# An attention and feed-forward stack on one core: the stages in another order on every engine

## What is computed

```
for i in range(DEPTH):                      # 6
    x = attn_layer(shift_tokens(x), Wqkv[i], q_scale[i], k_scale[i], Wo[i]) + x
    x = ffn_layer(shift_tokens(x), ln_g[i], ln_b[i], W1[i], b1[i], W2[i], b2[i]) + x

# attn_layer: 16 heads of 64; q, k are normed to length 1, scaled, rotated
sim = einsum('bhwie,bhwje->bhwij', bq, bk2) * 8        # 32 queries against 64 keys
attn = softmax(where(mask, -max, sim))
out = einsum('bhwij,bhwje->bhwie', attn, bv2)          # then out @ Wo
# ffn_layer: layer norm, hg = xn @ W1 + b1 (2 x 341 columns), a * gelu(gate) @ W2 + b2
```

## Time and profile before

| | |
|---|---|
| median of 3 runs | 3269.31 us (3269.1 to 3272.2) |
| the profiled execution, its own time | 3271.82 us |
| its span | 3270.0 us |
| PE busy | 3202.3 us, 98% |
| DVE busy | 2647.7 us, 81% |
| ACT busy | 2431.3 us, 74% |
| POOL busy | 2213.2 us, 68% |

### The profile page before, as it was taken

The page is one execution under the profiler, slowest core; times in us unless marked ns, Lnnn a source line. Parts: engine busy times, 40 slices in busy tenths (PEclk is TensorE's granted clock), DMA queues, the critical chain, the costliest instruction groups (busy, mean ns, idle before and its releaser), DMA issues. The chain is left out here.

```text
span 3270.0 us, 149708 instructions
## 1 busy us (share of the span) xinstructions
PE 3202.3 (98%) x62645; PEld 2538.3 (78%) x62645; DVE 2647.7 (81%) x6351; ACT 2431.3 (74%) x5028; POOL 2213.2 (68%) x1332
## 2 busy tenths in 40 slices
PE   7889999999999999999999999999999999999997
PEld 5668877877887887787787788778788778778875
DVE  5658888878888887888888888888888888888884
ACT  3347777777777777777777778778777777777774
POOL 5448767766776776676776677677677667767762
PEclk9989999999999999999999999999999999999999
DMA  4431111221211131111122111122111122112111
GB/s 160 161 128 51 45 43 43 55 88 48 56 46 42 47 98 48 53 45 43 46 87 63 48 50 46 38 82 71 49 44 48 43 62 87 53 45 53 50 45 37
DMA packets 110574, 200.00 MB, mean 61 GB/s; under 512 B 19280, under 2 KB 40784, under 8 KB 109136
## 3 DMA queue, kind: packets, MB, share of 16 engines
q1 hardware_dynamic: 107168, 185.17, 19.6%
q10 hardware_dynamic: 2736, 5.25, 0.5%
HBM read 41.45 MB, written 23.07 MB: 20 GB/s over the span
## 5 line engine op out<-in xcount | busy, mean ns | idle before, releaser
L438 POOL TENSOR_TENSOR qks<-work 128x1024 f32<-128x1024 f32 x384 | 909.9, 2370 | 134.9 <-issue 125.5
L446 POOL TENSOR_TENSOR qkr<-qks,rnorm 128x1024 f32<-128x1024 f32 x384 | 731.5, 1905 | 310.4 <-issue 223.0
L789 PE MATMUL psum<-wparts,xhi 128*128 128x512 f32 x2304 | 821.8, 438 | 11.9 <-POOL xlo L423 7.0
L573 ACT ACTIVATE sq<-psum 128x512 f32<-128x512 f32 x768 | 459.9, 599 | 301.4 <-PE psum L789 280.4
L454 POOL TENSOR_TENSOR probn<-prob,psumr 128x512 f32<-128x512 f32 x384 | 401.5, 1046 | 370.7 <-DVE psumr L1170 370.5
L1119 DVE TENSOR_REDUCE ssq<-sq 128x8 f32<-128x512 f32 x768 | 519.9, 677 | 4.3 <-ACT sq L573 4.2
L1146 DVE TENSOR_TENSOR work<-psum,rot 128x512 f32<-128x512 f32 x768 | 509.1, 663 | 1.8 <-POOL qks L438 1.8
L814 PEld LDWEIGHTS psum<-kT,qTs 64*32 64x32 f32 x24576 | 360.5, 107 | 145.2 <-issue 129.8
L789 PEld LDWEIGHTS psum<-wparts,xhi 128*128 128x128 f32 x2304 | 384.7, 191 | 101.2 <-issue 50.2
L789 PE MATMUL psum<-wparts,xlo 128*128 128x512 f32 x1152 | 459.7, 399 | 0.0
L1164 DVE TENSOR_REDUCE psumr<-prob 128x8 f32<-128x512 f32 x384 | 261.7, 682 | 243.4 <-ACT prob L625 240.8
(11 more groups left out here) (132 smaller groups left out, 5536.7 us busy)
## 6 DMA issues: line engine op xcount, KB each, us to landing
vsh<-vtok SPq DMA_DIRECT2D x384, 192.0 KB, 2.4
vsh<-vtok SPq DMA_DIRECT2D x384, 64.0 KB, 2.4
wsplit<-wstage SPq DMA_DIRECT2D x15, 1024.0 KB, 6.4
wparts<-wsplit SPq DMA_DIRECT2D x30, 512.0 KB, 3.9
xsh<-xs_in SPq DMA_DIRECT2D x192, 64.0 KB, 2.4
ff_x<-x_mid SPq DMA_DIRECT2D x96, 128.0 KB, 2.4
wraw<-Wqkv_dram SPq DMA_DIRECT2D x18, 512.0 KB, 4.3
rsplit<-rstage SPq DMA_DIRECT2D x5, 1024.0 KB, 3.8
```

The source lines that it names most:

```text
L438: pool.tensor_tensor(qks[:, :, :], rcos, rsin, ALU.add).then_inc(s["add_ready"], 1)
L446: pool.tensor_tensor(qkr[:, n % 2, :, :], qks[:, :, :], rnorm[:, :].unsqueeze(2).to_broadcast([P, 2 * OCT, DH]), ALU.mult).then_inc(s["qkr ...
L573: act.activation(sq[:, w * OCT:(w + 1) * OCT, :], bank[w].rearrange("p (h n) -> p h n", n=DH), ACT.Square).then_inc(s[("sqq_ready", "sqk_r ...
L789: mm = pe.matmul(out, xparts[xp][:, ti, :], wparts[:, SECTION_AT[w, oc], wp_, :], start=(k == 0), stop=(k == 2))
```

## The change

On all engines the loop calls its stages in another order, and some stages serve a unit one step later. On PE a step was: Q product, scores, turn Q, turn probabilities, K product, V product, turn K, attend, output. It becomes: turn Q, Q product, turn probabilities, K product, V product, turn K, scores, attend, output. `attend` and `output` are one step later. `ffn_tokens` moves from place 1 to place 2 and `ffn_features` stays at place 2 and so stands behind tokens, scores, attend and output of the same step; `ffn_up` stays at place 3 but moves from the step's end to behind the Q product; `ffn_down` moves from place 4 to place 7, between V product and turn K. `block_at` is rewritten so that a place may be 8 or more, and the loops run 8 steps longer. The waits' numbers follow the new distances; no wait is of a new kind. No instruction is added or dropped, but for a few rows that merge.

```diff
 def block_at(step, place):
-    b = step // UNROLL - 2
-    return b if step % UNROLL == place and 0 <= b < DEPTH * BLOCKS else None
+    b = (step - place) // UNROLL - 2
+    return b if (step - place) % UNROLL == 0 and 0 <= b < DEPTH * BLOCKS else None
...
-            x_low(0)
             global_inverse(2 * B - 1)
...
-            for step in range(STEPS + 2 * UNROLL):
-                if step:
-                    x_low(step)
-                probabilities(step - 5)
-                rotated(step - 1)
-                normed(step - 1)
+            for step in range(STEPS + 3 * UNROLL):
+                x_low(step - 2)
+                probabilities(step - 8)
+                rotated(step - 3)
+                normed(step - 3)
...
-            for step in range(STEPS + 2 * UNROLL):
-                ffn_renewed(renewed_at(step, 15))
-                mask_seeded(step - 3)
-                ffn_inverse(block_at(step, 2))
+            for step in range(STEPS + 3 * UNROLL):
+                ffn_renewed(renewed_at(step, 16))
+                mask_seeded(step - 4)
+                square(step - 1, 1)
+                values(step - 4)
+                ffn_inverse(block_at(step, 3))
                 x_high(step)
+                exponential(step - 5)
                 k_turned(step - 3)
-                attended(step - 6)
-                ffn_gates(block_at(step, 4))
                 ffn_affine(block_at(step, 3))
-                exponential(step - 4)
+                attended(step - 7)
+                q_turned(step - 2)
+                ffn_gates(block_at(step, 3))
+                inverse_norm(step - 1)
                 square(step, 0)
-                inverse_norm(step - 1)
-                q_turned(step - 2)
-                probabilities_turned(step - 5)
-                square(step, 1)
-                values(step - 3)
+                probabilities_turned(step - 6)
...
-            for step in range(STEPS + 2 * UNROLL):
+            for step in range(STEPS + 3 * UNROLL):
+                turn_q(step - 2)
                 projection(step, 0)
-                scores(step - 3)
-                turn_q(step - 2)
-                turn_probabilities(step - 5, (block_at(step, 2), "f_no", lambda b: b + 1), (block_at(step, 3), "f_xnT", lambda b: b + 1),
-                                   (block_at(step, 4), "f_u", lambda b: b * CH + 1), (block_at(step, 5), "f_out", lambda b: b + 1),
-                                   (last_block_at(step, 7), "yo_ready", lambda k: k + 1))
+                ffn_up(block_at(step, 3))
+                turn_probabilities(step - 6, (block_at(step, 3), "f_u", lambda b: b * CH + 1), (block_at(step, 8), "f_out", lambda b: b + 1),
+                                   (last_block_at(step, 10), "yo_ready", lambda k: k + 1))
                 projection(step, 1)
                 value_projection(step - 3)
+                ffn_down(block_at(step, 7))
                 turn_k(step - 2)
-                ffn_tokens(block_at(step, 1))
-                turned_back(last_block_at(step, 6), step)
-                attend(step - 5, block_at(step, 4))
+                ffn_tokens(block_at(step, 2))
+                turned_back(last_block_at(step, 9), step)
+                scores(step - 3)
+                attend(step - 6, block_at(step, 3))
+                output(step - 7)
                 ffn_features(block_at(step, 2))
-                ffn_down(block_at(step, 4))
-                output(step - 6)
-                ffn_up(block_at(step, 3))
...
-            for step in range(STEPS + 2 * UNROLL):
-                inverse_sum(step - 5)
+            for step in range(STEPS + 3 * UNROLL):
+                square_sum(step - 1, 1)
+                inverse_sum(step - 6)
+                ffn_out(block_at(step, 8))
+                scaled(last_block_at(step, 9))
+                added(last_block_at(step, 10))
+                guarded(step - 1)
+                rotation(step - 1, 1)
+                probability_sum(step - 5)
+                residual(step - 8)
+                row_maximum(step - 4)
+                below_maximum(step - 4)
+                ffn_gated(block_at(step, 3))
+                square_sum(step, 0)
                 ffn_statistics(block_at(step, 2))
-                scaled(last_block_at(step, 6))
-                added(last_block_at(step, 7))
-                rotation(step - 1, 1)
+                rotation(step, 0)
                 ffn_normed(block_at(step, 2))
-                square_sum(step - 1, 1)
-                ffn_out(block_at(step, 5))
-                residual(step - 7)
-                guarded(step - 1)
-                probability_sum(step - 4)
-                ffn_gated(block_at(step, 4))
-                row_maximum(step - 3)
-                square_sum(step, 0)
-                below_maximum(step - 3)
-                rotation(step, 0)
```

More of the change, by code:

```diff
@@ L318, in stored @@
                 sp.dma_start(out_v[k], yout[:, :, :]).then_inc(s["y_sent"], 16)
-            for step in range(STEPS + 2 * UNROLL):
+            for step in range(STEPS + 3 * UNROLL):
                 x_half(step)
                 section_renewed(renewed_at(step, 0), SECTION_AT[1, 1])
-                ffn_fetched(block_at(step, 1))
+                ffn_fetched(block_at(step, 2))
                 values_shifted(step - 4)
-                stored(last_block_at(step, 7))
+                stored(last_block_at(step, 10))
                 rotation_renewed(renewed_at(step, -6), 0)
@@ L332, in _ @@
                 rotation_renewed(renewed_at(step, 2), 1)
-                output_renewed(renewed_at(step, 6))
+                output_renewed(renewed_at(step, 7))
             sp.wait_ge(s["y_sent"], 16 * BLOCKS)
@@ L855, in value_projection @@
                     pe.wait_ge(s["gout_ready"], 2 * B)
-                if n % 2:
-                    need(pe, "x_mid_ready", (n - 4 + 1) // UPT)
+                if n % 2 == 0:
+                    need(pe, "x_mid_ready", (n - 4) // UPT)
                 project(bank[5], n, 2).then_inc(s["vp_ready"], 1)
@@ L883, in output @@
                 need(pe, "aot_ready", n + 1)
-                need(pe, "vs_ready", min(n + 4, STEPS))
+                need(pe, "vs_ready", min(n + 5, STEPS))
                 need(pe, "x_mid_ready", tile)
@@ L897, in ffn_tokens @@
                 need(pe, "f_out", b)
-                need(pe, "pts_ready", min(b * UNROLL + 2 * UNROLL + 1 - 4, STEPS))
+                need(pe, "yo_ready", b - (DEPTH - 1) * BLOCKS)
+                need(pe, "pts_ready", min(b * UNROLL + 2 * UNROLL + 2 - 5, STEPS))
                 for i in range(TPI):
@@ L906, in turned_back @@
                 pe.wait_ge(s["y_ready"], k + 1)
-                need(pe, "pts_ready", min(step - 4, STEPS))
+                need(pe, "pts_ready", min(step - 5, STEPS))
                 for i in range(TPI):
@@ L915, in ffn_features @@
                 pe.wait_ge(s["f_no"], b + 1)
-                need(pe, "pts_ready", min(b * UNROLL + 2 * UNROLL + 2 - 4, STEPS))
                 for i in range(TPI):
@@ L927, in ffn_up @@
                 pe.wait_ge(s["f_xnT"], b + 1)
-                need(pe, "pts_ready", min(step - 4, STEPS))
+                need(pe, "pts_ready", min(step - 6, STEPS))
                 for ch in range(CH):
@@ L932, in ffn_up @@
                         need(pe, "f_u", b * CH)
-                        need(pe, "aot_ready", min(step - 4, STEPS))
+                        need(pe, "aot_ready", min(step - 6, STEPS))
                     pe.matmul(bank[FFN_BANKS[ch]][0:w, :], w1[:, DFF + ch * P:DFF + ch * P + w], ff_n[:, :],
@@ L946, in ffn_down @@
                 pe.wait_ge(s["f_u"], b * CH + CH)
-                need(pe, "pts_ready", min((b + 2) * UNROLL + 4 - 4, STEPS))
+                need(pe, "pts_ready", min((b + 2) * UNROLL + 7 - 5, STEPS))
                 for ch in range(CH):
```

## The result

The changed kernel takes **3484.13 us** (median of 4 runs, 3474.8 to 3491.6), the kernel before 3270.47 on the same chip (4 runs, 3269.1 to 3272.2). The ratio is 1.0653, 95% interval 1.0639 to 1.0668: slower, and far outside the predicted range. The profiled execution has a span of 3475.2 us against 3270.0, so 205 us have to be found, and about 50 more that the forecast had expected to be saved.

What follows compares the result with a forecast made beforehand. PE's own row of instructions was taken to bound the kernel. -64 (group costs), +14 (gelu wait) and +3 (ends) gave -47, 3225 us from the profile, 3222 from the median; forecast 3226, eight in ten 3174 to 3264.

Steps and rivals of the forecast that it cites:

- Where PE could wait now: Check of PE's waits for late engines or transfers: only the gelu wait counted, 14 us; no wait in a plain unit.
- What a group costs behind another: Passages between array-wide and small-piece groups on PE: 0.14 us saved per unit, with transposes behind attend 64 us together.
- the value of 0.13: Passage from scores' to attend's pieces on PE: taken to cost 0.13 us, like coming out of attend.
- the free passage: Rival: scores to attend costs nothing extra, starts 0.90 us apart, another 50 us goes, 3177 us; chance 0.22.
- Array-wide groups neutral among themselves: PE's transposes and projections, up and down: a new order among themselves costs nothing.
- the sum of -47: Whole kernel: -64 from group costs, +14 from the gelu wait, +3 at the ends, against the profiled 3271.82 us.
- The wait for the first gelu: Behind the gates, PE waits for ACT's table load and first gelu: 0.3 us per block, 14 us in 48.
- Features do not wait: FFN features behind tokens, scores, attend and output: the norm is ready in time by 0.08 us, nothing counted.
- Turn Q behind the copy of K: Head of a plain unit: turn Q needs bank 2 emptied by ACT's copy of K; margin 0.1 us, no wait.
- The rival that ends on the slower side: ACT becomes the limit at turn Q in units without output: +77 us, 3303 us; chance 0.12.
- The period: Sign of being right: about 61.5 us between the gates of two blocks.
- PE over 97% busy: Sign of being right: PE still busy for over 97%, so without new waits of weight.

Runs made afterwards that it cites:

- the moved stream: Changed kernel with 64 small products more ahead of TensorE's loop, so later records stand half a block of 256 later: 3460.91 us, ratio 1.059.
- placed: Changed kernel, gelu table and mask early, scores and attend taken apart in 163 units where a 256-record boundary falls 26 to 132 records behind attend's first: 3384.29 us.
- misplaced edits: Control: table and mask early, scores and attend taken apart in 163 units where no boundary falls 20 to 134 records behind attend's first: 3480.47 us.

## Why the prediction was wrong

- **The step that failed** is "Where PE could wait now", and ahead of it the sentence that a change of order can act in two ways only: by what a group costs behind another, or by making PE wait. For each wait I asked which engine or transfer is late, and came to no wait in a plain unit. PE's own instruction stream was not on the list. It costs 164 us in attend itself, and 85 us more lie in the other groups: 54 of them in groups at the lower clock behind a stall, most of the rest in further gaps, 17 of which are such stalls in the output projection and turn Q. That the stalls come from the instruction stream is shown by the moved stream, the halved scores, and the stalls of the placed and misplaced edits.
- **What a group costs behind another** held in every median. Scores' start to attend's start is 1.03, as written under "what would show it", so the passage drains (the value of 0.13; the free passage, 0.90, is out). Summed over the medians of its groups, a plain unit with output went from 7.63 to 7.48 us and one without from 5.85 to 5.65, 68 us in 384 units where 64 were forecast. Turn K or tokens to scores is 0.53:

```profile
1285.09 0.60 PE L899 MATMUL psum<-ident,ff_x 128*128 128x128 f32 x4
1285.62 1.10 PE L812 MATMUL psum<-kT,qTs 64*32 64x64 f32 x64
1286.65 0.32 PE L871 MATMUL psum<-probT,vsh 64*64 64x32 f32 x8
...
1287.71 2.05 PE L887 MATMUL psum<-aoT,wo 128*128 128x128 f32 x16
...
1289.60 0.60 PE L916 MATMUL psum<-ident,ff_x 128*128 128x128 f32 x4
```

- **Array-wide groups neutral among themselves**: held where the same pair of groups occurs in both (turned probabilities to projection 0.58, projection to projection 0.69, projection to turn K 0.56). The span without the excess is 3226, the sum of -47 on the span of before gives 3223; since the 7 us of excess in the kernel before are in the one and not in the other, the sum was good to about 10 us, and most of the 64 us were there.
- **The wait for the first gelu**: right in kind, a little small. 0.38 us per block instead of 0.3, 18 us instead of 14. ACT's row in one block, to compare with the earlier trace rows, shows the load directly ahead of the gelu, and PE waits for it:

```profile
1292.01 1.28 ACT L646 ACT_TABLE_LOAD   x1
1293.31 1.83 ACT L650 ACTIVATE gel<-psum,b_col 128x512 f32<-128x512 f32 x3
```

- **Features do not wait**: held in this block and in all but one (margin 0.08; the features start 1.89 after the output, no gap). It goes when PE gets faster: in the run with halved scores the features come 0.3 us later behind the output.
- **Turn Q behind the copy of K** did not become the limit: 4.8 us in 5 waits. The rival that ends on the slower side had the right sign with the wrong mechanism, which is luck. The unit without output adds up to 5.67 and not to the 5.6 of the prediction, so the margin there was nearer 0.2 than 0.1. It was small all the same: 152, 36, 64 and 84 waits in the runs that made V or the scores later.
- **The period** between two blocks' gates was to be 61.5 us; it is 66.3 in the median (62.51 before). **PE over 97% busy**: 93%.

A sign of it could have been read beforehand. In the kernel before, attend has one such gap:

```profile
2729.47 0.30 PE L873 MATMUL psum<-probT,vtok 64*64 64x32 f32 x8
2730.60 0.32 PE L873 MATMUL psum<-probT,vsh 64*64 64x32 f32 x8 [0.84 <-issue]
```

A wait for "issue" in the middle of a group without a semaphore, and a queue of instruction packets whose number, 499, is PE's record count over 256, were both in the trace.

**What stays open.** Why the next block's packet starts a median 38 records past the boundary in the kernel before, 45 with the scores behind the next projection, 63 with doubled scores, 86 with the mask early and 97 in the changed kernel. The longer row by itself may explain some of it (more records pass in the same time), the wait for the mask at its head some more; I have not separated these. Nor does a boundary in the critical place always stall: 109 of 149 do. It is also open why the clock fell after 28 of the 111 stalls and not after the others, and no edit brought the saved time back.

## What to carry to other kernels

Before putting groups of many small products side by side, count PE's instructions: where some 160 or more follow at 8 ns each, the next block of 256 instructions may come too late, at about 1.3 us of idle time a stall (141 us in 113), and what came behind (the lower clock, further gaps) added half as much again here. The length of the row alone does not decide: in the old order a row of 256 stalled in 1 unit of 10. A model of PE that adds up group costs needs this as its own line, beside the semaphores and the drains. A wait for "issue" inside a group that has no semaphore is its mark, and its place modulo 256 told it here from the waits for other engines.

## What the runs showed of the hardware that was not expected

- TensorE's instructions come in blocks of 256 (499 packets of 16 KB for 127,812 records). From a packet's start to the first instruction behind a stall it takes 2.48 us, while the packet itself takes 1.1.
- Two groups of 128 records at 8.0 ns each stalled in 111 of 384 units, single ones between array-wide groups in 1. 0.59 us more between them shortened the stalls by about 0.5.
- 64 small products ahead of a loop move every stall of attend to other units and leave their number nearly as it is (111 and 105).
- A stall can cost twice: one of 3.1 us is followed by 5 us at a granted clock of 0.50. The clock fell after 28 of the 111 stalls in attend.
